# Pair attention: ScalarE's queue issues the twelve loads of the second unit when its program begins

## The reference, cut to what matters

```python
h = jnp.concatenate([x, latents], axis=1)          # x: the context, latents: the state
q = (latents @ q_w + q_b).reshape(b, k_len, NH, DH)             # NH = 16 heads, DH = 16
kv = (h @ kv_w + kv_b).reshape(b, p + k_len, NH, DH, 2)
kmat, v = (kv[..., 0], kv[..., 1])
attn = jnp.einsum('bkhd,bnhd->bhkn', q, kmat) / DH
attn = jnp.where(full_mask[:, None, None, :], attn, -jnp.inf)
attn = jax.nn.softmax(attn, axis=-1)
attn_out = jnp.einsum('bhkn,bnhd->bkhd', attn, v).reshape(b, k_len, H)
```

## Time and profile before

| | us |
|---|---|
| median of 3 runs | 1305.93 (1305.92 to 1308.3) |
| the profiled execution | 1308.49 |
| its span, first to last instruction | 1306.7 |
| TensorE matmuls busy | 1211.3 (93%) |
| VectorE busy | 968.6 (74%) |
| ScalarE busy | 736.1 (56%) |
| GpSimd busy | 507.3 (39%) |

### The profile page before, as it was taken

The page is one execution under the profiler, slowest core; times in us unless marked ns, Lnnn a source line. Parts: engine busy times, 40 slices in busy tenths (PEclk is TensorE's granted clock), DMA queues, the critical chain, the costliest instruction groups (busy, mean ns, idle before and its releaser), DMA issues. The chain is left out here.

```text
span 1306.7 us, 27356 instructions
## 1 busy us (share of the span) xinstructions
PE 1211.3 (93%) x9144; PEld 1000.9 (77%) x9144; DVE 968.6 (74%) x2179; ACT 736.1 (56%) x1670; POOL 507.3 (39%) x670
## 2 busy tenths in 40 slices
PE   5999999999799999999889879999899999499989
PEld 4999999999699999999769735558677778255578
DVE  5878787887788788778785468947488876589474
ACT  5665655766466656567662237764166664077651
POOL 4645455444474454554041000122299970001040
PEclk9999999999899999999989959999999999589899
DMA  5210011010211101110030697220384003876021
GB/s 176 58 34 15 27 32 32 24 32 1 101 34 34 33 9 32 32 32 8 1 101 2 129 106 87 41 83 25 89 197 85 2 10 72 127 81 83 2 69 33
DMA packets 56534, 70.90 MB, mean 54 GB/s; under 512 B 6864, under 2 KB 47572, under 8 KB 54104
## 3 DMA queue, kind: packets, MB, share of 16 engines
q1 hardware_dynamic: 54832, 65.83, 24.7%
q10 hardware_dynamic: 1600, 3.76, 1.0%
HBM read 46.79 MB, written 8.13 MB: 42 GB/s over the span
## 5 line engine op out<-in xcount | busy, mean ns | idle before, releaser
L932 ACT ACTIVATE a_prob<-a_s_ps,a_negmax 128x257 f32<-128x257 f32 x256 | 119.0, 476 | 92.8 <-DVE a_negmax L1014 92.8
L2156 DVE TENSOR_REDUCE s_mx<-s_s_ps 128x2 f32<-128x1024 f32 x128 | 152.0, 1211 | 18.3 <-PE s_s_ps L2201 17.9
L2141 ACT ACTIVATE s_probT<-s_st_ps 128x512 f32<-128x512 f32 x256 | 132.2, 606 | 57.7 <-PE s_st_ps L2215 55.4
L873 POOL TENSOR_TENSOR x_v_hi<-a_v_sum,x_one 128x512 fp32r<-128x512 f32 x60 | 63.2, 1054 | 243.8 <-DVE a_v_sum L1003 243.8
L1938 POOL TENSOR_SCALAR s_below<-s_masked,s_mx 128x256 f32<-128x256 f32 x256 | 117.8, 480 | 4.0 <-DVE s_mx L1966 3.1
L1029 DVE TENSOR_TENSOR a_pT_lo<-a_t_ps,a_pT_hi 128x512 fp32r<-128x512 f32 x128 | 88.2, 689 | 37.2 <-ACT a_pT_hi L945 35.5
L1014 DVE TENSOR_REDUCE a_negmax<-a_s_ps 128x2 f32<-128x514 f32 x128 | 86.8, 688 | 23.0 <-PE a_s_ps L1075 22.9
L945 ACT ACTIVATE a_pT_hi<-a_t_ps 128x512 fp32r<-128x512 f32 x128 | 76.7, 599 | 46.7 <-PE a_t_ps L1129 43.1
L2278 POOL TENSOR_TENSOR a_k_high<-x_tok,parts_b_out 128x256 f32<-128x256 f32 x16 | 11.1, 731 | 229.3 <-DMA parts_b_out<-L_xattn_out_b 229.3
L1966 DVE CUSTOM_DVE_ANT_0 s_masked<-s_s_ps,l_mask 128x256 f32<-128x256 f32 x256 | 90.7, 420 | 4.5 <-PE s_s_ps L2003 4.5
L2201 PE MATMUL s_s_ps<-l_k_st,l_q_st 49*128 49x512 f32 x192 | 68.1, 546 | 22.2 <-PEq L2506 10.2
(11 more groups left out here) (348 smaller groups left out, 4039.3 us busy)
## 6 DMA issues: line engine op xcount, KB each, us to landing
a_wo_raw<-L_xattn_wo SPq DMA_DIRECT2D x16, 256.0 KB, 3.3
x_wqk_raw<-L_xattn_wq SPq DMA_DIRECT2D x31, 128.0 KB, 2.3
x_wqk_raw<-L_xattn_wk SPq DMA_DIRECT2D x31, 128.0 KB, 2.3
x_wv_raw<-L_xattn_wv SPq DMA_DIRECT2D x15, 256.0 KB, 3.1
l_k_st<-k_second SPq DMA_DIRECT2D x12, 256.0 KB, 9.8
l_k_st<-k_stack SPq DMA_DIRECT2D x16, 192.0 KB
l_q_st<-q_stack SPq DMA_DIRECT2D x12, 192.0 KB
x_vbias<-L_xattn_bias_v SPq DMA_DIRECT2D x2, 1024.0 KB, 6.5
```

The costliest lines, as they stand in the source:

```text
L932: nc.scalar.activation(prob[:, n % 2, qt, 0:NK], s_ps[:, n % 2, qt, 0:NK], ACT.Exp, bias=negmax[:, n % 2, qt:qt + 1], accum_out=den[:, n % ...
L2141: nc.scalar.activation(probT[:, third % 2, n // 4, n // 2 % 2, n % 2], st_ps[:, u % 3], ACT.Exp, scale=c.scale).then_inc(z.exp_done, 1)
L2156: nc.vector.tensor_reduce(mx[:, i % 2, qt, a::2], s_ps[:, n % 2], AX.X, ALU.max).then_inc(z.max_done, 1)
```

## The change: who issues the second unit's loads

The twelve loads of the second unit leave the sync queue's rounds 0 and 1. ScalarE issues all twelve, keys first, at the start of its list in pair attention, ahead of its first round. Tiles, sizes and the semaphore stay as they are. The sync queue keeps the copies of the rows of maxima and the loads of the third and the fourth unit. Both layer 1 and layer 3 run this code.

```diff
@@ pair_attention, block.sync @@
                             sp.dma_start(slots[g % 3][0][m:m + 1, :, b].bitcast(F32),
                                          mxT[2 * half:2 * half + 2, second % 2].bitcast(F32)
                                          ).then_inc(row_in[second % 2], 16)
-                    if first in (0, 1):
-                        second_unit.load(c, sp, first == 0, slots[1][first == 0], unit_in[0])
                     if first is not None and 2 <= first <= 5:
                         late.load_head(c, sp, 2, first - 2, *slots[2], unit_in[1])
@@ pair_attention, block.scalar @@
                             wait(act, z.x_done, fourth)
                             nc.scalar.activation(oT[:], o_ps, ACT.Copy).then_inc(z.o_out, 1)
+                for is_k in (True, False):
+                    second_unit.load(c, act, is_k, slots[1][is_k], unit_in[0])
                 rounds(body)
```

## The result

The changed kernel took 1318.44 us (median of 5 runs, 1313.39 to 1319.0), the one before 1306.56 us in the runs beside it (5 runs, 1305.92 to 1308.3). The ratio is 1.0065, with a 95% interval of 1.0036 to 1.0094: slower, where 1303.5 was predicted and 1307.5 was the upper end. (The quotient of the two medians is 1.0091, within the interval.) The profiled execution of the changed kernel took 1318.46 us.

The account below looks back on a forecast made before the run. TensorE, busy 93% of the span, was taken as the bound, with gaps of 5.4 and 5.2 us waiting for quad 0's row. (2.4 - 1.1) + (2.2 - 1.1) = 2.4 us off 1305.93 gave 1303.5 us, range 1297.9 to 1307.5.

Parts of the forecast that it names:

- queues take turns load by load: Quad 0's row, alone on its queue, passes the key loads after 1.7 to 4.0 us; likeliest case, 41 in 100.
- The DMA engines had key loads in hand until about 763, so the query loads don't finish earlier for it.: Query loads queue behind the key loads from about 752.5 instead of 758.5 us, without finishing earlier.
- The gain of 2.4 and 2.2 us: TensorE's wait for quad 0's row shortens by 2.4 us in layer 1 and 2.2 in layer 3.
- The loss of 1.1 us a stage: Quad 1's row, issued near 765.4 us, meets query loads still running until about 770: 1.1 us lost per stage.
- the 0.7 us of PEld's second wait: TensorE's weight loads wait 0.7 us more in layer 1, a wait that quad 1's row ends.
- ScalarE's issues at 0: Twelve issues on ScalarE's queue take 5.4 to 6.0 us, covered by 15.4 us of idle time: price 0.
- The rival in which that queue holds the engine: Slow issues on ScalarE's queue delay its exponentials: 6.5 us slower, 1312.4 us; 9 in 100.
- The 3.3 us of a row without loads in its way: From a row's first issue to its matmul, without load traffic: at most 3.3 us (767.87 to 771.21).
- The second unit's landing: Second unit's last loads land at 775 or so, against a need near 778 at quad 4: no loss.
- gains nothing: Quad 0's row still comes about when it does today: 0 to 1 us gained, 1305.4 us; 28 in 100.

Follow-up runs that it names:

- the kernel with the smallest waits for rows: Loads paced behind the rows, third unit's constant rows in round 3; against that kernel, one key load less ahead of quad 1's row: 1302.41 us, ratio 0.9972.

## Why the prediction was wrong

**The step that failed** is the one on which the gain rested: "So I take it that queues take turns load by load." The runs show order of issue across both queues in its place: a row alone on its queue waits for six key loads on the other just as it does behind them (5.6 and 5.9 us), and for twelve, 10.2 to 11.0 us, in either assignment of queues. In the changed kernel its packets move only after 765.7 us, more than 10 us after its issue at 755.07.

**Where it was misread.** The opening's rows bear both rules. ScalarE's load issued at 1.22 us landed at 6.5, and the sync queue's 512 KB load, issued at 0.74, landed at 5.9 between the two. I took that for a turn. But the sync queue's load was also issued ahead of it, at 0.74 against 1.22. That ScalarE's first load, begun at 0.75, landed before it, at 3.1, doesn't speak against order of issue either: an issue takes time, 0.44 us for that load and 0.73 for the sync queue's:

```profile
0.74 0.73 SPq L316 DMA_DIRECT2D ctxT<-ctx_turned  x1
```

The three issues end at 1.19 (ScalarE), 1.47 (sync) and 1.70 (ScalarE), and the loads land in that order. With both queues equally busy, turns and order of issue give the same landings. A row that separates the two needs a late, small issue on an empty queue beside a full one, and before has none.

**"The DMA engines had key loads in hand until about 763, so the query loads don't finish earlier for it."** True, and it should have been followed one step on: the query loads don't finish earlier, but from where they stand now, ahead of the row, the row finishes later. The prediction costed their move at 0; by order of issue it is six loads at 0.95, 5.7 us, measured 5.0 and 5.5.

**The gain of 2.4 and 2.2 us** for quad 0: measured a loss of 5.0 and 5.5. **The loss of 1.1 us a stage** at quad 1's row: none, since everything has landed by then; the 0.7 us of PEld's second wait is gone as well.

**ScalarE's issues at 0:** right. They took 6.3 us, 747.74 to 754.07, and 7.2 in layer 3, against 5.4 to 6.0 estimated, and ended before the predicted 757, in a stage that began 2 us earlier; 14 us of idle time cover the excess. The rival in which that queue holds the engine did not occur, though its sign was right: 1312.4 for another reason.

**The 3.3 us of a row without loads in its way** were not that: the matmul at 771.21 started as the last query load landed, near 771.1. In the kernel with the queries first, the row of quad 0 goes out with all loads nearly through, at 754.91, and its matmul starts 2.9 us later with no wait.

**The second unit's landing:** its last load lands at 769.0 in layer 1; nothing waits for it at quad 4, as said.

**The rivals:** "gains nothing" is what was measured, but in the kernel with only the key loads moved (1.0008). The rule of the Trainium skill behind that rival (page "DMA: Bandwidth & Descriptors", section "Queues, rings and completion order": an engine serves the queues in rotation and leaves one only after a whole packet) doesn't describe these runs, unless a packet were longer than twelve loads: in rotation a row alone on its queue would wait for one packet of the other, and here each load issued ahead of it adds its whole time, up to the twelfth. The same page of the Trainium skill, section "Issuing engines are not separate DMA queues", held up: it says that a second issuing engine saves only the time of issuing, and moving the key loads gave 1.0008. None of the rivals had a longer wait for the row, which is why the range missed.

**The size.** 10.5 us of waits, 10.0 of span, but the near agreement is partly chance. The changed kernel's profiled execution reaches layer 1's stage 2.1 us earlier, with no change before it. From there to layer 3's stage it takes 7.9 us more for 5.0 us of wait; TensorE's matmuls are busy 3.0 us longer there (345.1 against 342.1, 2960 of them in both), at a granted clock of 0.92 against 0.93. From layer 3's stage to the end it takes 4.2 us more for 5.5 us of wait. The medians differ by 11.9 us, and the ratio's interval, 1.0036 to 1.0094, is 5 to 12 us; the excess of the median is within the spread.

## What to carry to other kernels

Moving large transfers to another engine's queue doesn't take them out of a small one's way; what counts is what has been issued by any engine before it. List the transfers in order of issue, with their bytes, and ask of each urgent one how much stands ahead and when that will be through: here one landing row (4.4 us, then 2.3 and 0.95 a load) gave seven other starts within 1.1 us. Hand out prefetches in portions behind the urgent transfer of each round, and check what the portions push back.

## What the runs showed of the hardware

Transfers issued on the sync queue and on ScalarE's queue were served in the order of their issue. The experiments vary queue, order and bytes, but don't show where in the chip the order is kept. A second queue gave no bandwidth either. The kernel with the key loads on ScalarE's queue and the query loads on the sync queue tells. From the first issue to the last landing of the twelve loads, 748.8 to 770.3 us there and 749.8 to 771.2 before, the DMA traffic reads:

```profile
DMA packets 609, 2.52 MB, mean 117 GB/s; under 512 B 200, under 2 KB 208, under 8 KB 400
```

```profile
DMA packets 609, 2.52 MB, mean 118 GB/s; under 512 B 200, under 2 KB 208, under 8 KB 400
```

And a wait removed isn't always time won: in the kernel with the smallest waits for rows, TensorE ran at 1.2 GHz from 783 to 786 us, 2 us behind a wait of only 0.5, which took back what the last edit had gained in that stage.
